# Softmax stage of a graph network: two products back to back, and a quarter of the numerators on GpSimd

## The reference

```python
w_m = (efeat @ W_msg + b_msg).reshape(E, in_f, -1)
w_a = (efeat @ W_attn + b_attn).reshape(E, in_f, -1)
h_src = feat[src][:, :, None]
e1 = w_m * h_src
e2 = w_a * h_src
seg_max = jax.ops.segment_max(e2, dst, num_segments=N)
ex = jnp.exp(e2 - seg_max[dst])
denom = jax.ops.segment_sum(ex, dst, num_segments=N)
attn = ex / denom[dst]
ft = jax.ops.segment_sum(e1 * attn, dst, num_segments=N)
return ft.sum(axis=1)
```

## Time and profile before

| | |
|---|---|
| median of three runs | 9752.3 us (9752.12 to 9757.57) |
| profiled execution | 9742.4 us, span 9740.6 us |
| busy in the span | PE 8099.5, DVE 7316.8, POOL 6838.5, PEld 4287.6, ACT 3030.7 us |
| mean granted TensorE clock | 0.927 |
| softmax stage | from about 3050 to 6432 us |

### The profile page before, as it was taken

How to read it: one execution, slowest core, us unless ns; L and a number is a source line. 1 busy time by engine, 2 the same in 40 slices (tenths; PEclk the granted TensorE clock), 3 DMA queues, 4 the chain that set the end, 5 groups by cost and what they waited for, 6 DMA issues and landing times.

```text
span 9740.6 us, 132710 instructions
## 1 busy us (share of the span) xinstructions
PE 8099.5 (83%) x37269; PEld 4287.6 (44%) x37269; DVE 7316.8 (75%) x12995; ACT 3030.7 (31%) x12664; POOL 6838.5 (70%) x5177
## 2 busy tenths in 40 slices
PE   0899996999994888888888888846999995899994
PEld 0466663555551333333333333323655553555552
DVE  1566663444545999999999999987878785788884
ACT  0111111000004777777777777742000000000000
POOL 5688885777767766666666666636888887688887
PEclk6899996999996999999999999977999997999997
DMA  1333432222223777777777777766322221333332
GB/s 32 99 102 102 109 100 54 59 68 69 61 54 89 205 202 202 203 205 205 204 203 202 203 205 206 204 184 181 79 73 78 73 75 43 104 102 99 100 106 47
DMA packets 821262, 1215.28 MB, mean 125 GB/s; under 512 B 236715, under 2 KB 686344, under 8 KB 800376
## 3 DMA queue, kind: packets, MB, share of 16 engines
q1 hardware_dynamic: 573062, 996.22, 32.9%
q0 software_dynamic: 212624, 110.62, 9.8%
q10 hardware_dynamic: 35440, 106.85, 3.3%
HBM read 419.84 MB, written 787.23 MB: 124 GB/s over the span
## 4 chain that ended last, share of the span: by engine, by line
PE 41%; POOL 27%; ACT 17%; issue 9%; DVE 4%; DMA 2%; SPq 1%; DVEq 0%; ACTq 0%; POOLq 0%
POOL arena L567 27%; PE PS L958 21%; ACT arena L781 14%; PE PS L1124 5%; PE PS L1125 4%; PE PS L980 4%; PE PS L1093 2%; PE PS L1094 1%; ACT arena L822 1%; PE PS L941 1%; DVE arena L1878 1%; PE PS L1085 1%; PE PS L1077 1%; PE PS L1087 1%; ACT arena L800 1%
## 5 line engine op out<-in xcount | busy, mean ns | idle before, releaser
L958 PE MATMUL PS<-arena,TB 125*128 125x500 bf16 (+1 forms) x18711 | 4066.0, 373 | 106.2 <-DVE arena L1402 93.2
L567 POOL DMA_INDIRECT arena<-d_feat,srci x1650 | 2116.1, 1282 | 1249.2 <-ACT arena L781 765.8
L958 PEld LDWEIGHTS PS<-arena,TB 125*128 125x128 bf16 x18711 | 1832.2, 99 | 2009.4 <-issue 170.0
L567 POOL DMA_INDIRECT arena<-d_h,srci x1485 | 1932.8, 1302 | 610.3 <-issue 442.0
L781 ACT ACTIVATE arena<-PS,arena 125x32 f32<-125x32 f32 x10560 | 2011.9, 445 | 354.9 <-PE PS L1077 228.0
L1402 DVE TENSOR_SCALAR arena<-arena,lane 125x2000 bf16<-125x2000 f16 (+2 forms) x1848 | 1224.1, 721 | 364.9 <-PE PS L958 241.3
L1414 DVE SCALAR_TENSOR_TENSOR arena<-arena,lane,PS 128x500 f32<-128x500 f16 x891 | 637.2, 715 | 1101.4 <-PE PS L958 947.8
L567 POOL DMA_INDIRECT arena<-d_rel,irel x858 | 1208.4, 1408 | 306.2 <-issue 261.2
L567 POOL DMA_INDIRECT arena<-d_nn,srci x759 | 1069.5, 1409 | 283.3 <-issue 230.4
L1124 PE MATMUL PS<-arena,ident 125*125 125x512 f32 x1650 | 961.1, 665 | 314.1 <-DVE arena L1706 211.6
L1125 PE MATMUL PS<-arena 125*125 125x512 f32 x1650 | 885.7, 620 | 0.0
(11 more groups left out here) (278 smaller groups left out, 7227.6 us busy)
## 6 DMA issues: line engine op xcount, KB each, us to landing
d_smax<-arena SPq DMA_DIRECT2D x165, 1120.0 KB
d_sums_low<-arena SPq DMA_DIRECT2D x330, 560.0 KB
d_sums_high<-arena SPq DMA_DIRECT2D x330, 560.0 KB
arena<-d_pick SPq DMA_DIRECT2D x66, 843.8 KB
arena<-d_lane SPq DMA_DIRECT2D x66, 843.8 KB
d_x<-arena ACTq DMA_DIRECT2D x165, 241.7 KB
arena<-d_x SPq DMA_DIRECT2D x165, 241.7 KB
d_rel<-arena SPq DMA_DIRECT2D x50, 669.4 KB
```

The source lines that it names most:

```text
L567: gp.indirect_dma_start(out=dst, out_offset=None, in_=table, in_offset=bass.IndirectOffsetOnAxis(ap=index, axis=0)).then_inc(S(sem), 16)
L958: ins = pe.matmul(PS[:, acc_at(L, q):acc_at(L, q) + w], TB[:, part, g * LANES * F:(g + 1) * LANES * F], OH[L][i][:, g, at:at + w], start=g ...
```

## The change

VectorE's multiplication for steps 6 to 9 shrinks to steps 6 and 7. Steps 8 and 9 of block b − 4 are multiplied by GpSimd (`last_numerators`), in its stream behind the third gather of block b, once the first exponentials of that block are done and `top` 0 of the block after it. The row sum of step 8 and ScalarE's reuse of `PB` wait for it (`soft_gp_num`). In VectorE's order the third product moves up to stand right behind the second, and from there on the work of block o comes one or two places earlier. A semaphore of the set-up (`wct_c`) is replaced by a further count of another (`wa`), and late sums (after the last block) take two steps where they took four.

```diff
--- before.py
+++ after.py
@@ -612,6 +612,16 @@
             gp.wait_ge(S("tab_conv2"), 16 * NT)
             narrow("conv2")
 
+            def last_numerators(b):
+
+                s = b % 3
+                gp.wait_ge(S("soft_exp"), 6 * b + 1)
+                if b < NB1 - 1:
+                    gp.wait_ge(S("soft_max"), MAXES * (b + 1) + 1)
+                rows = XD[:, s, B1 - 2:B1, :]
+                gp.tensor_tensor(paired(rows, 1), paired(PB[:, s, NA - 2:NA], 1), paired(rows, 0), ALU.mult)\
+                    .then_inc(S("soft_gp_num"), 1)
+
             gp.wait_ge(S("tab_soft"), 16 * NT)
             for b in range(NB1):
                 s = b % 3
@@ -619,10 +629,14 @@
                     gp.wait_ge(S("soft_ap"), NA * (b - 2))
                 for t in range(AT, B1):
                     gather(GH[:, s, t, :], d_feat, srci[:, b * B1 + t:b * B1 + t + 1], f"soft_late_g{s}")
+                    if b >= 4 and t == B1 - 2:
+                        last_numerators(b - 4)
                 for t in range(AT):
                     if b >= 3 and t % 2 == 0:
                         gp.wait_ge(S("soft_prod"), NG3 * (b - 3) + t // 2 + 1)
                     gather(GH[:, s, t, :], d_feat, srci[:, b * B1 + t:b * B1 + t + 1], f"soft_g{s}")
+            for b in range(NB1 - 4, NB1):
+                last_numerators(b)
             for s in range(3):
                 gp.wait_ge(S(f"soft_s{s}"), 160 * THIRD)
             for a, table in enumerate((d_smax, *d_sums)):
@@ -776,6 +790,7 @@
                     act.wait_ge(S(f"soft_late_g{s}"), 16 * NA * (k + 1))
                     if not isinstance(b, int) or b >= 3:
                         act.wait_ge(S("soft_num"), 4 * (b - 2))
+                        act.wait_ge(S("soft_gp_num"), b - 2)
                 bank = (4 + n % 2) * 512
                 for i in range(F):
                     ins = act.activation(PB[:, s, n, 2 * F * i:2 * F * (i + 1)], PS[0:P, bank + 2 * F * i:bank + 2 * F * (i + 1)],
@@ -904,7 +919,7 @@
             pe.matmul(PS[:, 3584:3585], foldt[:, :], small[0:F, 20:21], start=True, stop=True).then_inc(S("gate_v"), 1)
 
             pe.transpose(PS[0:NB, 2048:2048 + R], small[0:R, 32:32 + NB], ident[0:R, 0:R]).then_inc(S("wct"), 1)
-            pe.wait_ge(S("wct_c"), 1)
+            pe.wait_ge(S("wa"), 3)
             pe.matmul(PS[0:R, 2560:2560 + F * F], small[0:NB, 480:480 + R], small[0:NB, 64:64 + F * F],
                       start=True, stop=True).then_inc(S("wrel_p"), 1)
 
@@ -1312,7 +1327,7 @@
             link(v.tensor_copy(gdst[:, :], PS[0:P, 1536:1536 + F]))
             link(v.tensor_copy(fold[:, F:TW], PS[:, 3584:3585]))
             dve.wait_ge(S("wct"), 1)
-            v.tensor_copy(small[0:NB, 480:480 + R], PS[0:NB, 2048:2048 + R]).then_inc(S("wct_c"), 1)
+            v.tensor_copy(small[0:NB, 480:480 + R], PS[0:NB, 2048:2048 + R]).then_inc(S("wa"), 1)
             dve.wait_ge(S("wrel_p"), 1)
             v.tensor_copy(small[0:R, 640:640 + F * F], PS[0:R, 2560:2560 + F * F]).then_inc(S("wrel"), 1)
             v.tensor_scalar(diag[:, :], ident[0:P, 0:P], one_run[:, 0:1], None, ALU.mult).then_inc(S("diag"), 1)
@@ -1741,6 +1756,8 @@
                 else:
                     if t in (2, 4, 6):
                         dve.wait_ge(S("soft_num"), 4 * b + t // 2 + 1)
+                    if t == B1 - 2:
+                        dve.wait_ge(S("soft_gp_num"), b + 1)
                     dve.wait_ge(S("soft_sum"), (B1 - 2) * b + t - 1)
                 v.scalar_tensor_tensor(to, last, KR[:, s, t, 1:2], to, ALU.mult, ALU.add).then_inc(S("soft_sum"), 1)
 
@@ -1760,7 +1777,7 @@
                 row_sum(b, s, 2)
                 row_sum(b, s, 3)
                 weigh(b, s, 4, 2)
-                weigh(b, s, AT, NA)
+                weigh(b, s, AT, NA - 2)
                 for t in range(4, B1 - 1):
                     row_sum(b, s, t)
 
@@ -1782,33 +1799,33 @@
                 dve.wait_ge(S(f"soft_k{s}"), 16 * (k + 1))
                 top(b, s, 0)
                 product(b, s, 1)
+                product(b, s, 2)
                 top(b, s, 1)
                 top(b, s, 2)
-                product(b, s, 2)
                 top(b, s, 3)
+                weigh(o, z, 0, 2)
                 top(b, s, 4)
-                weigh(o, z, 0, 2)
+                carry(o, z)
                 top(b, s, 5)
-                carry(o, z)
+                weigh(o, z, 2, 2)
                 top(b, s, 6)
+                row_sum(o, z, 1)
                 top(b, s, 7)
-                row_sum(o, z, 1)
                 top(b, s, 8)
-                weigh(o, z, 2, 2)
+                row_sum(o, z, 2)
                 top(b, s, 9)
-                row_sum(o, z, 2)
+                row_sum(o, z, 3)
                 top(b, s, 10)
-                row_sum(o, z, 3)
+                weigh(o, z, 4, 2)
                 top(b, s, 11)
-                weigh(o, z, 4, 2)
+                row_sum(o, z, 4)
                 top(b, s, 12)
-                row_sum(o, z, 4)
+                weigh(o, z, AT, NA - 2)
                 top(b, s, 13)
-                weigh(o, z, AT, NA)
+                row_sum(o, z, 5)
                 top(b, s, 14)
-                row_sum(o, z, 5)
+                row_sum(o, z, 6)
                 top(b, s, 15)
-                row_sum(o, z, 6)
                 top(b, s, 16)
                 if left >= 1:
                     first_product(b + 1, (s + 1) % 3, k + (s == 2))
```

## The result

| | before | after |
|---|---|---|
| median of the runs, us | 9752.2 (9744.2 to 9757.6, 4 runs) | 9891.7 (9879.5 to 9898.3, 4 runs) |
| profiled execution, span, us | 9740.6 | 9889.5 |
| granted clock, mean of the span | 0.927 | 0.905 |
| `carry` of block 10 / of block 160, us | 3271.2 / 6355.9 | 3291.0 / 6499.5 |

The changed kernel takes 1.0145 times as long (interval 1.0131 to 1.0159): **slower by some 140 us**, far outside the forecast range. Of the 148.9 us between the two profiled spans, 19.8 arise before the `carry` of block 10, 123.8 over the next 150 blocks and 5.3 behind them. The cost recurs block by block; the start is a small part. The period of a block is, from here on, the time from its `carry` to the next one.

The account below looks back on a forecast made before the run. VectorE and a ScalarE-TensorE ring were taken as nearly equal bounds. Profiled execution: 9742.4 + 11.5 + 2 − 14 − 0.5 = 9741.4 us; being 9.9 us under the median, this gave 9751 us, range 9715 to 9810.

Parts of the forecast that it names:

- the ring: Closed chain of waits between ScalarE and TensorE, claimed to hold a block at 20.46 us, 0.10 under the present period.
- 0.39 and 0.12 us: VectorE per block: 0.39 us of waiting before the first row sum goes; a fourth pair of adjacent `top`s adds 0.12.
- TensorE's clock: Rival: changed waits at lower clock cost 0.35 us a block over half the blocks, +57 us, 9815 us; chance 15%.
- VectorE alone 19.75 us: VectorE's own work per block after the change: 20.56 − 0.54 − 0.39 + 0.12 us.
- GpSimd's multiplication 1.2 us, free beside the products: GpSimd's multiplication of 512 elements takes 1.2 us and, beside VectorE's two products, makes nothing wait.
- The start +13.5 us: First blocks: +11.5 us once for block 0's late GpSimd multiplication, +2 while GpSimd catches up.
- The 2 us for multiplications beside two-input instructions: For 4 to 9 early blocks GpSimd's late multiplication meets VectorE's two-input instructions: 0 to 4.5 us, taken as +2.
- nothing but two waits stands in front of VectorE's groups: VectorE's groups wait only 24.3 us for TensorE's first sum and 0.5 us for a store, in 112 blocks.
- 22% for slower: Chance of a slower kernel, given to the third and fourth rivals and a start costing 8 us more.
- the fourth rival: GpSimd's multiplication outlasts its place and holds VectorE's two-input instructions; at 3.5 us, +111 us, 9863 us; chance 7%.

Follow-up runs that it names:

- the one exchange in the kernel before: Kernel before with row sum 3 placed ahead of `top` 10 on VectorE, nothing else: 9915.7 us, ratio 1.0172.
- The combined kernel: Changed kernel plus `top`s early, the ring cut, ten added matmuls, and VectorE multiplying the last numerators of blocks 0 and 1: 9653.7 us, ratio 0.9906.
- `top`s early: Changed kernel with row sums 3 to 6 each behind a later `top`, so `top` 10 comes one row sum earlier: 9755.3 us, ratio 1.0008.
- doubled: Changed kernel with GpSimd's multiplication done twice per block, the first into a scratch tile: 9899.0 us, ratio 1.0159.
- the six matmuls: Changed kernel with six extra 512-column matmuls per block ahead of TensorE's first difference, into the bank it overwrites: 9753.4 us, ratio 1.0011.
- the ring cut: TensorE's product for ScalarE's next scaling issued ahead of the last sum: changed kernel 1.0167, with the six matmuls 1.0007; kernel before 0.9996.
- GpSimd's part alone: Kernel before, VectorE's order kept, with GpSimd multiplying the numerators of the last two steps: 9784.5 us, ratio 1.0039.

## Why the prediction was wrong

- **The failed step** is in its first part: "No link of it names VectorE. The one place where VectorE touches it is the fourth difference". Right of the ring, but the ring isn't the only closed path, and the working went on as if it were. The change's moves were costed by VectorE's idle time alone (0.39 and 0.12 us); what they do to `top` 10, 0.77 us later behind `carry` (one `top` and one row sum more ahead of it), was never worked out, though TensorE waits for that `top` in every block. In its place the runs showed a loop from `carry` over `top` 10 and the six differences to the next `carry`: 20.35 us with a short low stretch in the old order, 21.12 in the new one. A low stretch takes 1.14 us more in this loop (2.5 when long), and the cover for it fell from 0.2 us to less than nothing. That `top` 10's place alone does it is shown by the one exchange in the kernel before (ratio 1.0172).
- **The rival that came true** is TensorE's clock, with its place and its sizes wrong. It put the longer wait behind the first sum; it lies before the first difference (1.30 to 1.64 us). It said half the blocks; it is 138 in 154. It said 0.7 us by the ring; it is 0.50 for the short stretch and 1.88 for one of 6.8 us, a kind that none of these periods had before. Its +57 us became about +125, and its time of 9815 us is 77 us under the measured one. The prediction gave it 15%, and lists the sign that came, a clock clearly under 0.97, among the signs of being wrong.
- *VectorE alone 19.75 us*: right within 0.1. The combined kernel, which has VectorE as its only bound and the same number of close pairs, takes 19.85.
- *The ring 20.46 us*: right. 20.46 with `top`s early, 20.52 in the changed kernel's periods without low stretch; where it is cut, 19.98.
- *GpSimd's multiplication 1.2 us, free beside the products*: right, 1.29 to 1.30; doubled, it costs at the start alone.
- *The start +13.5 us*: too small. The one wait is 10.03 us, against 11.5 worked out. With `top`s early, where low stretches are few, the first ten blocks take 222.7 us, against 205.7 in the kernel before: +17, as the first five blocks stay long (31.97 to 21.35 us). The 2 us for multiplications beside two-input instructions were the small term. In the changed kernel three such instructions are held beside one, 5.1 us in all: two `top`s take 1.78 and 2.50 us in place of 0.48, a row sum 2.51 in place of 0.75. With `top`s early it is five instructions and 7.4 us, and the wait is 10.47 us: together 17.9, less the 1 us that ten periods of 20.46 gain.
- *Two slips without weight.* The prediction says that nothing but two waits stands in front of VectorE's groups; 21.7 us more stand in front of the `top`s (L1702), but much the same stands there in the changed kernel (20.9 and 3.8 us). And its 22% for slower is the third and the fourth rival alone, with nothing left for the longer start that it names.
- The forecast 9751 is near what the change measures where low stretches don't come or don't cost: ratio 1.0011 with the six matmuls, 1.0008 with `top`s early. That doesn't make it right.

## What to carry to other kernels

Where several engines are nearly balanced, write down every closed path that returns to the same instruction one block later, not only the one that the waits name now, and work out for each moved instruction how far it shifts the start of another engine's run, counted from the instruction that closes the path. Look at slow stretches that cost nothing: their cover (here 0.2 us) is part of the design, and the change may use it up. When TensorE's clock falls at a recurring idle place, first bring forward what it waits for; a few matmuls into a bank that is overwritten test the suspicion in one run, though they don't always keep the clock up (67 of 154 periods here had a low stretch in spite of them, with the ring cut). And look at the mean clock of all executions, not of the traced one alone: with `top`s early it went from 0.907 to 0.935 at the same time.

## What the runs showed of the hardware

- The granted clock falls around the start of TensorE's longest run, behind its wait for `top` 10: in the changed kernel from 0.97 us ahead of the first difference to 0.78 us behind its start. In the traced executions the low stretches number 3 in 154 blocks with a wait of 1.12 us, 49 with 1.30, 138 with 1.64. But the wait isn't all: with 2.18 us in the old order and the ring cut there were 80, and the kernel with 1.12 us had mean clocks from 0.907 to 0.935 in ten executions. Why the clock falls in one block and not in the next isn't shown.
- Low stretches come as 3.4 or 6.8 us in the clock's records. The long ones are many (39 to 51 blocks) only where the first difference starts 6.1 us behind `carry` and no matmuls were added, and one costs more than twice a short one.
- GpSimd's multiplication of 512 elements (1.30 us) holds a VectorE instruction with two operands in SBUF until 0.29 us after its end (78 `top`s of the run with GpSimd's part alone; one took 1.65 us in place of 0.48), and leaves a product that reads PSUM and one operand in SBUF alone (1.21 us).
